# A graph-network pair on one core: x in a ring of four slots, loaded three groups ahead, the residual written over x, and the next group's statistics behind the second layer's

## The chip, the cores and the metric

One Trainium2 chip, one of its cores. The metric is the device time of one execution in microseconds (us); the kernel is timed in several runs, and one more execution is profiled. Engines: PE (TensorE, matmul and its weight loads PEld), DVE (VectorE), ACT (ScalarE), POOL (GpSimd) and SP (SyncE, which here only issues DMAs).

## The reference, cut to what matters

x is 128 graphs x 128 nodes x 512 features, float32; adj is one 128x128 0/1 matrix.

```
h   = relu(layernorm(x))
z_l, z_g = h @ W_lang.T, h @ W_grav.T
A_l = relu(cosine similarity of the rows of z_l) * not_eye
A_g = exp(-squared distance of the rows of z_g / (2 sigma^2)) * not_eye
K   = w * rows_to_sum_1(A_l * adj) + (1 - w) * rows_to_sum_1(A_g * adj)
x   = x + (K @ (h @ W_V.T)) @ W_O.T                    # first layer, with the residual
h   = relu(layernorm(x))
x   = x + adjacency-weighted sum of h over nodes + bias # second layer
```

## The kernel before, in words

Four graphs are a group (GB = 4), so there are 32 groups (NG). Every product is done in three passes on pairs of rounded parts (hi, lo), so each engine that empties a PSUM bank works in two steps: ACT copies the bank to the hi part, and DVE subtracts hi from the bank to make the lo part (`lo`, L553; the names y_lo, v_lo and hT_lo below are such subtractions). One iteration i of every engine's loop does, in PE's order:

1. **y**: eight products (60 matmuls of 512 columns) with h of group i against the Gram matrices of W_lang and W_grav, through a ring of four PSUM banks (`free` waits on `drained`, which DVE counts up); in front of the last, the transposes of K of group i-1.
2. **KV**: K times v of group i-1, 12 matmuls; DVE adds x to them (`residual`, L621, `add`, L629) and takes the layer norm's statistics (`stats`, L633).
3. **P**: 48 matmuls of 256 columns, similarities of group i, into p_ps; ACT copies it out in two halves (L434).
4. **v**: 48 matmuls, four banks; ACT copies (v_hi, L446), DVE makes v_lo. Between them ACT and DVE split h of the next group, which came back transposed (turned_hi, L401; turned_lo, L573: hT_lo). Behind b = 0 DVE sums the diagonal (sq, L723; sqc, L725), ACT shifts four tiles (L479), and behind b = 2 PE has transposed P and DVE adds it (L738).
5. **layer 1** (the second layer) of group i-1: four products of three matmuls; each waits for its h2_lo. DVE adds x_out to each bank (`output`, L675).

The order on each engine is written out by hand; there is no planner. Each engine waits on semaphores only, and runs its list in order. The b-th item of a name is written name(b) here.

POOL's list in an iteration: norm1 of group i+1 (ten small ops, L271 to L285), add_bias(0) and (1) of group i-1 (L295: x_out = x2 + bias, waits for the statistics bn2 of its b), norm2 of group i-1 (the same ten ops, waits for all four bn2), `diagonal` (L309: P_sb times a mask; waits for ACT's two copies of P), add_bias(2) and (3), row_norms (L315, L317), four h2_lo (L302: h2f minus h2_hi). ACT's h2_full (L467) makes h2f from x2 behind norm2's last op; h2_copy (L474) is h2_hi.

The statistics of x (`x_stats`, L558, bn_stats L565) are taken two groups ahead, by DVE in the v phase: for b 0 and 1 behind sqc, for b 2 and 3 behind hT_lo(1). The last two groups have none to take (`stats=False`, `after=False`).

x is loaded by SP into a ring of three slots, two groups ahead (`load_x(i + 2)`, one DMA of 1 MB). In an iteration SP issues: half of the 16 DMAs that move h's 32x32 blocks (`turn_h`; ACT issues the other half, L395), the load, the two DMAs that spread the norms, and four stores. h itself is transposed in blocks of 32 by DVE (L569); the DMAs then bring the blocks to h_turned, 32 partitions and 16 runs of 128 bytes each; there a partition's 16 runs lie behind each other, and the readers pick them with a strided pattern (`h_columns`).

Before the loop, the four weights are loaded into tiles that are free at that time: W_lang into x2, W_V into the ring's last slot.

## Time and profile before

| | us |
|---|---|
| three runs | 1314.11, 1312.95, 1311.78 (median 1312.95) |
| the profiled execution | 1311.88, of which the span of the profile 1310.1 |
| busy: PE, PEld | 1261.6, 1036.9 |
| busy: DVE, ACT, POOL | 1032.7, 704.4, 661.8 |
| granted clock of PE | 0.993 of full |
| moved by DMA | 112.55 MB, mean 86 GB/s |

A busy PE row counts matmuls that overlap in the pipeline. "Busy" is from the first part of the page; the chain of waits (fourth part, and a view of its own) goes from the last instruction back to what released it. In the views in order of time a line is: start in us from the span's start, duration in us, engine, line of the kernel, operation, output<-inputs, their shapes, how many instructions are merged in the line, and in brackets the idle time of the engine in front of it with what ended it. An engine's next instruction can be issued a little before the one in front has ended (bn_stats of 0.68 follow each other every 0.60), and one that is issued but can't start counts as running. "issue" is time in which nothing is waited for that the profile shows. An engine name with a q (SPq, ACTq) is its sequencer.

### The profile page before, as it was taken

Reading aid. Unit: us, or ns where it says so; the run is one execution under the profiler, and the core shown is the slowest. Engines: PE = TensorE matmul, PEld = TensorE weight load, DVE = VectorE, ACT = ScalarE, POOL = GpSimd, SP = SyncE. Lnnn points to the kernel's source line nnn. Section 1 sums busy time; section 2 is a strip of 40 time slices with the busy share of each in tenths; the row PEclk is TensorE's granted clock in tenths of the full one; section 3 lists DMA queues with packets and bytes.
Section 4 is the critical chain, followed back from the end, with each engine's and each line's share of the span. In section 5 each row is a group of like instructions: output and inputs, shape, how many; then the busy total and the mean of one; then the engine's idle time right before and its main releaser. Section 6 shows DMA issues by size and latency. Waiting matters only on the chain.

```text
span 1310.1 us, 22323 instructions
## 1 busy us (share of the span) xinstructions
PE 1261.6 (96%) x6324; PEld 1036.9 (79%) x6324; DVE 1032.7 (79%) x1733; ACT 704.4 (54%) x1324; POOL 661.8 (51%) x995
## 2 busy tenths in 40 slices
PE   7899999999999999999999999999999999999996
PEld 7777888777888777888887878887888877788874
DVE  5487777797777788777788777789777779777778
ACT  5346555456555456645456655555655545655533
POOL 1025654545664445664444665444565454566434
PEclk9999999999999999999999999999999999999997
DMA  5312433432333332343332243342243342233211
GB/s 203 65 36 78 105 72 96 104 72 75 101 88 87 98 82 70 96 104 73 96 98 63 87 104 72 96 104 65 79 104 72 96 104 70 76 102 81 59 38 64
DMA packets 308894, 112.55 MB, mean 86 GB/s; under 512 B 269840, under 2 KB 269968, under 8 KB 308880
## 3 DMA queue, kind: packets, MB, share of 16 engines
q1 hardware_dynamic: 177360, 95.78, 25.5%
q10 hardware_dynamic: 131520, 16.60, 7.7%
q8 instruction: 7, 0.11, 0.0%
q14 instruction: 7, 0.06, 0.0%
HBM read 46.20 MB, written 33.62 MB: 61 GB/s over the span
## 4 chain that ended last, share of the span: by engine, by line
PE 64%; DVE 17%; issue 11%; ACT 6%; DMA 1%; DVEq 0%; POOL 0%; ACTq 0%; SPq 0%
PE ring L856 49%; PE p_ps L856 14%; DVE hT_lo L573 5%; DVE sq L723 3%; ACT v_hi L446 3%; ACT chain L479 3%; DVE bn L565 2%; DVE x_out L675 2%; DVE v_lo L553 1%; DVE chain L738 1%; PE kt_ps L869 1%; DMA h2f<-in_L_gnn_W_grav 1%; ACT h L383 0%; DVE bn L633 0%; DVE y_lo L776 0%
## 5 line engine op out<-in xcount | busy, mean ns | idle before, releaser
L295 POOL TENSOR_TENSOR x_out<-x,bias_sb 128x512 f32<-128x512 f32 x128 | 176.5, 1400 | 468.2 <-DVE bn L633 468.2
L410 ACT ACTIVATE y_hi<-ring 128x512 fp32r<-128x512 f32 x256 | 148.4, 591 | 230.2 <-PE ring L856 227.4
L856 PE MATMUL ring<-hT_hi,Lw_hi 128*128 128x512 f32 x640 | 256.5, 401 | 6.6 <-DVE hT_lo L573 2.1
L856 PE MATMUL ring<-hT_hi,Lw_lo 128*128 128x512 f32 x640 | 250.4, 391 | 0.0
L856 PE MATMUL ring<-hT_lo,Lw_hi 128*128 128x512 f32 x640 | 249.8, 390 | 0.0
L553 DVE TENSOR_TENSOR v_lo<-ring,v_hi 128x512 fp32r<-128x512 f32 x128 | 87.4, 684 | 201.0 <-ACT v_hi L446 197.2
L856 PE MATMUL ring<-MT_hi,hT_hi 128*128 128x512 f32 x512 | 202.8, 396 | 0.0
L856 PE MATMUL ring<-MT_hi,hT_lo 128*128 128x512 f32 x512 | 199.8, 390 | 0.0
L856 PE MATMUL ring<-MT_lo,hT_hi 128*128 128x512 f32 x512 | 199.8, 390 | 0.0
L302 POOL TENSOR_TENSOR h_lo<-h2f,h_hi 128x512 fp32r<-128x512 f32 x124 | 172.7, 1422 | 45.4 <-ACT h_hi L474 45.4
L553 DVE TENSOR_TENSOR y_lo<-ring,y_hi 128x512 fp32r<-128x512 f32 x256 | 169.3, 681 | 29.6 <-ACT y_hi L410 29.5
L434 ACT ACTIVATE chain<-p_ps 128x512 f32<-128x512 f32 x64 | 38.2, 598 | 241.0 <-PE p_ps L856 241.0
L856 PEld LDWEIGHTS ring<-hT_hi,Lw_hi 128*128 128x128 f32 x640 | 120.2, 188 | 47.6 <-DVE x_out L675 16.1
L856 PE MATMUL p_ps<-y_hi,hT_lo 128*128 128x256 f32 x512 | 145.0, 283 | 0.0
L856 PE MATMUL p_ps<-y_lo,hT_hi 128*128 128x256 f32 x512 | 145.0, 283 | 0.0
L856 PE MATMUL p_ps<-y_hi,hT_hi 128*128 128x256 f32 x512 | 144.9, 283 | 0.0
L856 PEld LDWEIGHTS ring<-hT_hi,Lw_lo 128*128 128x128 f32 x640 | 120.2, 188 | 26.2
L856 PEld LDWEIGHTS ring<-hT_lo,Lw_hi 128*128 128x128 f32 x640 | 120.4, 188 | 21.7
L573 DVE TENSOR_TENSOR hT_lo<-h_turned,hT_hi 128x512 fp32r<-128x512 f32 x124 | 127.4, 1027 | 0.0
L856 PEld LDWEIGHTS ring<-MT_hi,hT_lo 128*128 128x128 f32 x512 | 96.2, 188 | 20.6
L856 PEld LDWEIGHTS ring<-MT_lo,hT_hi 128*128 128x128 f32 x512 | 96.5, 188 | 17.9
L856 PEld LDWEIGHTS ring<-MT_hi,hT_hi 128*128 128x128 f32 x512 | 96.4, 188 | 18.0
(163 smaller groups left out, 2555.8 us busy)
## 6 DMA issues: line engine op xcount, KB each, us to landing
x_ring<-in_x SPq DMA_DIRECT2D x32, 1024.0 KB, 5.7
out<-x_out SPq DMA_DIRECT2D x128, 256.0 KB, 2.2
h_turned<-h SPq DMA_DIRECT2D x248, 64.0 KB, 2.1
h_turned<-h ACTq DMA_DIRECT2D x248, 64.0 KB, 2.1
rn_cols<-rn_dram SPq DMA_DIRECT2D x31, 256.0 KB, 3.7
x<-in_L_gnn_W_lang SPq DMA_DIRECT2D x4, 256.0 KB, 5.3
h2f<-in_L_gnn_W_grav SPq DMA_DIRECT2D x1, 1024.0 KB, 8.9
chain<-in_L_gnn_W_O SPq DMA_DIRECT2D x1, 1024.0 KB, 12.6
```

The source lines that it names most:

```text
L295: pool.tensor_tensor(x_out[:, b], x2[:, b], bias_sb[:, :], ALU.add).then_inc(x2b_ready, 1)
L302: pool.tensor_tensor(h2[1][:, b], h2f[:, b], h2[0][:, b].bitcast(F32), ALU.subtract)\
L410: act.activation(y[0][:, a, :, l], bank(n).rearrange("p (b m) -> p b m", b=GB), ACT.Copy)\
L434: act.activation(P_sb[:, 2 * half:2 * half + 2], p_ps[:, 2 * half:2 * half + 2], ACT.Copy)\
L446: act.activation(v[0][:, b], bank(n), ACT.Copy).then_inc(hi_ready, 1)
L479: e = act.activation(P_sb[:, b, 1], P_sb[:, b, 1], ACT.Identity, bias=sq[:, b, 1:2])
L553: return dve.tensor_tensor(out, ps, part(hi), ALU.subtract)
L565: dve.bn_stats(bn1[:, b], xb).then_inc(bn1_done, 1)
L573: dve.tensor_tensor(hT_columns(1, b), h_columns(b), part(hT_columns(0, b)), ALU.subtract)\
L675: dve.tensor_tensor(x_out[:, b], bank(n), x_out[:, b], ALU.add).then_inc(drained, 1)
L723: dve.tensor_reduce(sq[:, :, :], diag, AX.X, ALU.add).then_inc(sq_ready, 1)
L856: mm = pe.matmul(out, lhsT, rhs, start=(k == 0), stop=(k == len(terms) - 1))
```

## The change

The ring of x gets a fourth slot, and group i+3 is loaded in iteration i, behind the stores. The residual is written over x in its slot; the tile x2 is gone, and add_bias, h2_full and the statistics read the slot (`x_rows`, whose address is computed from the group number in a register). On DVE the statistics of x move from the v phase into `residual`: one between stats(1) and stats(2), three behind stats(3); `added` is the wait for an add, now its own function, put two adds later. W_lang is loaded into the ring's slot 2. h_turned is laid out as [b, c, m] like a tile of h, so that the block DMAs write runs of 128 bytes 512 bytes apart, and both readers have a plain pattern. The prologue's loads of x are written out. The diff, where "..." marks what is left out:

```diff
@@ -12,7 +12,7 @@
 P = 128
 Q = 32
 GB = 4
-SLOTS = 3
+SLOTS = 4
 BANKS = 4
 EPS_LN = 1e-5
 EPS = 1e-8
@@ -70,7 +70,6 @@
         P_sb, diag, A = (chain[:, n] for n in range(3))
         K = sb("K", [P, GB, P])
         KT = [sb(f"KT_{s}", [P, GB, P], F32R) for s in ("hi", "lo")]
-        x2 = sb("x2", [P, GB, D])
         x_out = sb("x_out", [P, GB, D])
         h2f = sb("h2f", [P, GB, D])
         h2 = [sb(f"h2_{s}", [P, GB, D], F32R) for s in ("hi", "lo")]
@@ -101,10 +100,10 @@
         deg = sb("deg", [P, 4, GB, 2])
 
 
-        h_turned = sb("h_turned", [P, NQ, C * GB * Q])
+        h_turned = sb("h_turned", [P, GB, C, P])
         h_blocks = h[:, :, :].rearrange("p b (c j q) -> p j (b c) q", c=C, j=NQ)
 
-        raw_l = x2[:, :, :]
+        raw_l = x_ring[:, SLOTS - 2]
         raw_g = h2f[:, :, :]
         raw_v = x_ring[:, SLOTS - 1]
         raw_o = chain[:, 0:2].rearrange("p a b l m -> p (a b l m)").rearrange("p (c n) -> p c n", c=C)
@@ -182,13 +181,17 @@
                 eng.wait_ge(sem, count)
 
         def h_columns(b):
-            return h_turned[:, :, :].rearrange("p i (b c q) -> p b c i q", c=C, b=GB)[:, b]
+            return h_turned[:, b]
 
         def turned_to(i, j):
-            return h_turned[j * Q:(j + 1) * Q, i].rearrange("p (e q) -> p e q", q=Q)
+            return h_turned[j * Q:(j + 1) * Q, :, :, i * Q:(i + 1) * Q].rearrange("p b c q -> p (b c) q")
 
         def hT_columns(part, b):
-            return hT[part][:, :, b].rearrange("p c (i q) -> p c i q", q=Q)
+            return hT[part][:, :, b]
+
+        def x_rows(g, b):
+
+            return x_ring[:, bass.ds(g % SLOTS, 1), b].rearrange("p s d -> p (s d)")
 
         block = ctx.enter_context(nc.Block())
 
@@ -218,20 +221,15 @@
                     for j in range(NQ):
                         sp.dma_start(turned_to(i, j), h_blocks[i * Q:(i + 1) * Q, j]).then_inc(turned, 16)
 
-            def iteration(i, load=True, store=True, after=True):
+            def iteration(i, load=True, after=True):
                 if after:
                     turn_h(i + 1)
-                if load:
-                    sp.wait_ge(x_loaded, 16 * i + 32)
-                    if store:
-                        sp.wait_ge(drained, first_use(i) + G_USES + GB)
-                    else:
-                        sp.wait_ge(w_split, 3 * C)
-                    load_x(i + 2)
                 if after:
                     spread_norms(i)
-                if store:
-                    store_out(i - 1, first_use(i) + PER - GB)
+                store_out(i - 1, first_use(i) + PER - GB)
+                if load:
+                    sp.wait_ge(x_loaded, 16 * i + 48)
+                    load_x(i + 3)
 
             w_rows = w_lang.rearrange("(c p) n -> p c n", p=P)
             for c in range(C):
@@ -242,10 +240,18 @@
             sp.dma_start(raw_v, w_v.rearrange("(c p) n -> p c n", p=P)).then_inc(w_loaded["v"], 16)
             sp.wait_ge(x_loaded, 16)
             load_x(1)
-            iteration(0, store=False)
+            sp.wait_ge(w_split, C)
+            sp.wait_ge(x_loaded, 32)
+            load_x(2)
+            turn_h(1)
+            spread_norms(0)
+            sp.wait_ge(w_split, 3 * C)
+            sp.wait_ge(x_loaded, 48)
+            load_x(3)
             iteration(1)
-            with sp.Fori(2, NG - 2) as i:
+            with sp.Fori(2, NG - 3) as i:
                 iteration(i)
+            iteration(NG - 3, load=False)
             iteration(NG - 2, load=False)
             iteration(NG - 1, load=False, after=False)
             store_out(NG - 1, first_use(NG) + GB)
@@ -292,7 +298,7 @@
                 if b == 0:
                     wait_for(pool, out_stored, 16 * GB * g)
                 pool.wait_ge(bn2_done, GB * g + b + 1)
-                pool.tensor_tensor(x_out[:, b], x2[:, b], bias_sb[:, :], ALU.add).then_inc(x2b_ready, 1)
+                pool.tensor_tensor(x_out[:, b], x_rows(g, b), bias_sb[:, :], ALU.add).then_inc(x2b_ready, 1)
 
             def norm2(g):
                 std_factors(g, bn2, bn2_done, ln2, ln2_step)
@@ -379,8 +385,7 @@
                     elif not isinstance(g, int) or g > 1:
                         act.wait_ge(turned, TURN * (g - 1))
                 for b in range(b0, b0 + GB // 2):
-                    xb = x_ring[:, bass.ds(g % SLOTS, 1), b].rearrange("p s d -> p (s d)")
-                    act.activation(h[:, b], xb, ACT.Relu, bias=ln1[:, SHIFT, b:b + 1],
+                    act.activation(h[:, b], x_rows(g, b), ACT.Relu, bias=ln1[:, SHIFT, b:b + 1],
                                    scale=ln1[:, RSTD, b:b + 1]).then_inc(h_ready, 1)
 
             def t_hi(b, n):
@@ -464,7 +469,7 @@
                     act.wait_ge(ln2_step, LN_STEPS * (g + 1))
                 if b == 0:
                     wait_for(act, h2_split, GB * g)
-                act.activation(h2f[:, b], x2[:, b], ACT.Relu, bias=ln2[:, SHIFT, b:b + 1],
+                act.activation(h2f[:, b], x_rows(g, b), ACT.Relu, bias=ln2[:, SHIFT, b:b + 1],
                                scale=ln2[:, RSTD, b:b + 1]).then_inc(h2_done, 1)
 
             def h2_copy(g, b):
@@ -561,8 +566,7 @@
                     dve.wait_ge(x_loaded, 16 * g + 16)
                     wait_for(dve, ln1_step, LN_STEPS * g)
                 for b in range(b0, b1):
-                    xb = x_ring[:, bass.ds(g % SLOTS, 1), b].rearrange("p s d -> p (s d)")
-                    dve.bn_stats(bn1[:, b], xb).then_inc(bn1_done, 1)
+                    dve.bn_stats(bn1[:, b], x_rows(g, b)).then_inc(bn1_done, 1)
 
             def turn_blocks(g, b):
                 dve.wait_ge(h_ready, GB * g + b + 1)
@@ -618,32 +622,42 @@
                 dve.wait_ge(kt_hi, g + 1)
                 dve.tensor_tensor(KT[1][:, :, :], kt_ps[:, :, :], part(KT[0][:, :, :]), ALU.subtract).then_inc(kt_split, 1)
 
-            def residual(g, n, use, last=False):
+            def residual(g, n, use, x_next=None, last=False):
 
                 wait_for(dve, h2_done, GB * g)
                 wait_for(dve, x2b_ready, GB * g)
 
                 def add(b):
-                    xb = x_ring[:, bass.ds(g % SLOTS, 1), b].rearrange("p s d -> p (s d)")
                     dve.wait_ge(kv_done, GB * g + b + 1)
-                    dve.tensor_tensor(x2[:, b], bank(n + b), xb, ALU.add).then_inc(drained, 1)
+                    dve.tensor_tensor(x_rows(g, b), bank(n + b), x_rows(g, b), ALU.add).then_inc(drained, 1)
+
+                def added(b):
+                    dve.wait_ge(drained, use + b + 1)
 
                 def stats(b):
-                    dve.wait_ge(drained, use + b + 1)
-                    dve.bn_stats(bn2[:, b], x2[:, b]).then_inc(bn2_done, 1)
+                    dve.bn_stats(bn2[:, b], x_rows(g, b)).then_inc(bn2_done, 1)
 
                 if last:
                     for b in range(GB):
                         add(b)
+                        added(b)
                         stats(b)
                         if b % 2 == 1:
                             last_factors(b - 1, b + 1, b // 2 * LAST_STEPS)
                     return
                 add(0)
-                for b in range(1, GB):
+                add(1)
+                for b in range(2, GB):
+                    added(b - 2)
                     add(b)
-                    stats(b - 1)
-                stats(GB - 1)
+                    stats(b - 2)
+                added(GB - 1)
+                if x_next is not None:
+                    x_stats(x_next, 0, 1)
+                for b in range(GB - 2, GB):
+                    stats(b)
+                if x_next is not None:
+                    x_stats(x_next, 1, GB)
 
             def last_factors(b0, b1, before):
 
@@ -701,11 +715,12 @@
                         if before and n == G_USES - 1:
                             kt_lo(i - 1)
                 if before:
-                    residual(i - 1, n, first_use(i) + n)
+                    residual(i - 1, n, first_use(i) + n, i + 2 if stats and after else None)
                 else:
                     for c in range(C):
                         hi += 1
                         lo(MT[1][:, c], bank(n + c), MT[0][:, c], hi).then_inc(drained, 1)
+                    x_stats(i + 2, 0, GB)
                 n += GB
                 if not after:
                     last_chain(i, n, hi)
@@ -723,8 +738,6 @@
                         dve.tensor_reduce(sq[:, :, :], diag, AX.X, ALU.add).then_inc(sq_ready, 1)
                         dve.wait_ge(sq_ready, 2 * i + 1)
                         dve.tensor_scalar(sqc[:, :], sq[:, :, 0], EPS * EPS, None, ALU.max).then_inc(sq_ready, 1)
-                    if stats and b < 2:
-                        x_stats(i + 2, b * GB // 2, (b + 1) * GB // 2)
                     if b == 2:
                         sum_s(i)
                 if before:
```

## Rows read from the trace of the kernel before

**Rows 1.** The page's first part: busy time, share of the span, instructions.

```profile
PE 1261.6 (96%) x6324; PEld 1036.9 (79%) x6324; DVE 1032.7 (79%) x1733; ACT 704.4 (54%) x1324; POOL 661.8 (51%) x995
```

**Rows 2.** The chain of waits: start us, us, what (the KV matmuls of two groups).

```profile
600.35 3.01 PE ring L856 x12
...
639.35 3.01 PE ring L856 x12
```

**Rows 3.** PE in order of time, end of layer 1, start of y.

```profile
661.51 0.49 PE L856 MATMUL ring<-h_hi,A_hi 128*128 128x512 f32 x1 [0.22 <-POOL h_lo L302]
...
662.76 0.49 PE L856 MATMUL ring<-h_hi,A_hi 128*128 128x512 f32 x1 [0.29 <-POOL h_lo L302]
...
663.32 0.40 PE L856 MATMUL ring<-h_hi,A_lo 128*128 128x512 f32 x1
663.84 0.50 PE L856 MATMUL ring<-hT_hi,Lw_hi 128*128 128x512 f32 x1
```

**Rows 4.** POOL in order of time, the same group.

```profile
648.53 0.20 POOL L285 TENSOR_TENSOR ln<-ln 128x4 f32<-128x4 f32 x1
648.82 2.40 POOL L309 TENSOR_TENSOR chain<-chain,diag_of 128x1024 f32<-128x1024 f32 x1
651.17 1.29 POOL L295 TENSOR_TENSOR x_out<-x,bias_sb 128x512 f32<-128x512 f32 x1
...
657.06 5.57 POOL L302 TENSOR_TENSOR h_lo<-h2f,h_hi 128x512 fp32r<-128x512 f32 x4 [1.33 <-ACT h_hi L474]
```

**Rows 5.** DVE in order of time, the same group's v phase.

```profile
652.13 0.89 DVE L573 TENSOR_TENSOR hT_lo<-h_turned,hT_hi 128x512 fp32r<-128x512 f32 x1
...
656.58 0.68 DVE L573 TENSOR_TENSOR hT_lo<-h_turned,hT_hi 128x512 fp32r<-128x512 f32 x1
657.18 1.28 DVE L565 BATCH_NORM_STATS2 bn<-x_ring 128x6 f32 x2
...
658.97 1.26 DVE L573 TENSOR_TENSOR hT_lo<-h_turned,hT_hi 128x512 fp32r<-128x512 f32 x1
...
661.88 1.30 DVE L573 TENSOR_TENSOR hT_lo<-h_turned,hT_hi 128x512 fp32r<-128x512 f32 x1
663.10 1.28 DVE L675 TENSOR_TENSOR x_out<-ring,x_out 128x512 f32<-128x512 f32 x2
```

**Rows 6.** ACT in order of time, the same group.

```profile
650.89 0.60 ACT L446 ACTIVATE v_hi<-ring 128x512 fp32r<-128x512 f32 x1 [0.60 <-PE ring L856]
```

**Rows 7.** DVE and POOL in order of time, the same group's residual and norm2.

```profile
644.15 1.28 DVE L633 BATCH_NORM_STATS2 bn<-x 128x6 f32<-128x512 f32 x2
...
645.51 0.21 POOL L271 TENSOR_TENSOR ln<-bn 128x4 f32<-128x4 f32 x1 [0.41 <-DVE bn L633]
```

**Rows 8.** DVE and POOL in order of time, group 1.

```profile
98.13 1.28 DVE L633 BATCH_NORM_STATS2 bn<-x 128x6 f32<-128x512 f32 x2
...
102.65 2.39 POOL L309 TENSOR_TENSOR chain<-chain,diag_of 128x1024 f32<-128x1024 f32 x1
...
105.83 1.01 DVE L573 TENSOR_TENSOR hT_lo<-h_turned,hT_hi 128x512 fp32r<-128x512 f32 x1
```

**Rows 9.** DVE and PE in order of time, iteration 30 (`stats=False`).

```profile
1237.26 0.90 DVE L573 TENSOR_TENSOR hT_lo<-h_turned,hT_hi 128x512 fp32r<-128x512 f32 x1
...
1243.77 1.61 DVE L573 TENSOR_TENSOR hT_lo<-h_turned,hT_hi 128x512 fp32r<-128x512 f32 x1
...
1249.07 0.47 PE L856 MATMUL ring<-hT_hi,Lw_hi 128*128 128x512 f32 x1 [0.22 <-DVE x_out L675]
```

**Rows 10.** Who waited for whom: us in total, times, longest.

```profile
DVE bn L565 <- issue: 5.7, 28, 0.2
```

**Rows 11.** The page's sixth part: DMA issues, KB each, us to landing.

```profile
x_ring<-in_x SPq DMA_DIRECT2D x32, 1024.0 KB, 5.7
...
h_turned<-h ACTq DMA_DIRECT2D x248, 64.0 KB, 2.1
```

**Rows 12.** ACT in order of time, its block DMAs.

```profile
639.42 5.46 ACTq L395 DMA_DIRECT2D h_turned<-h  x8
```

## The prediction

> **What bounds the kernel now.** The page's first part comes first: TensorE (PE) is busy 1261.6 of 1310.1 us [rows 1], so a change pays only where PE stands still, and costs only where it makes PE wait. The chain of waits shows the period: the same 12 KV matmuls start at 600.35 and at 639.35 [rows 2], so one group takes 39.0 us. From here on the group that starts at 639.35 is read; the others look alike.
>
> PE's own timeline [rows 3] shows where it stands still. Its matmuls of 512 columns follow each other every 0.23 us. The products of the second layer (layer 1 in the code) for b = 2 and b = 3, at 661.51 and 662.76, have idle time in front of them that POOL's h2_lo ended; the last matmul of b = 3 starts at 663.32, yet the next group's first y matmul only at 663.84, 0.29 later than a pitch of 0.23 would have it: it waits for the bank that DVE's first x_out add empties. From 662.76 to 663.32 two matmuls take 0.56 instead of 0.46, so a restart costs 0.10 more.
>
> What sets these waits is a chain that runs backwards through three engines, and the reader should follow it in [rows 4 to 6]:
> - ACT's v_hi of b = 0 at 650.89, then two DVE splits, of which the second, hT_lo(0), is issued at 652.13 and takes 0.89;
> - DVE's sum of the diagonal (sq), ACT's four shifts, ACT's v_hi, hT_hi and h2_hi, and POOL's four h2_lo from 657.06, 5.57 long, to 662.63;
> - hT_lo(3), issued at 661.88, 1.30 long, and x_out(0), issued at 663.10, 0.74 in front of the y matmul, and 0.68 long.
>
> hT_lo is the interesting row. It is the same instruction four times a group, and takes 0.89, 0.68, 1.26, 1.30 [rows 5]. At 0.68 POOL is idle. In the other three POOL is in a large op: the x_out add of b = 2 runs 651.17 to 652.46 [rows 4], and hT_lo, issued at 652.13, ends 0.56 after that add, about the 0.60 pitch of an unhindered op. So hT_lo(0) starts when POOL's add is over, and **the end of hT_lo(0) is tied to POOL**: an add that starts later by t makes the chain later by t. Going one step back, that add follows the diagonal product (648.82, 2.40), which follows norm2 (its last op issued at 648.53) and ACT's second copy of P.
>
> The Trainium skill, "SBUF — State Buffer", section "SBUF: two separate sides", says that Vector and GpSimd share one pair of SBUF ports as an exclusive lock: a DVE op with two SBUF inputs and a GpSimd op that reads SBUF never run together, and the loser waits for the whole instruction. The trace agrees (0.68 alone, 1.30 behind a POOL op). If the ports were shared by bandwidth instead, a later POOL op would not push hT_lo(0)'s end one for one, and the sum below would be near nothing.
>
> **The change part by part.**
>
> *Statistics out of the v phase.* Four bn_stats, two pairs of 1.28, leave the stretch behind sq and the stretch in front of v_lo(2). The first pair stands beside ACT's shifts, and v_lo(1) waits for ACT: worth nothing. The second pair, 657.18 to 658.46 [rows 5], is on the printed chain. Does DVE get ahead without it? Iteration 30, the last but one, never had these statistics (there is no group 32), so the trace of before already shows it: hT_lo(2) is issued there at 1243.77 and takes 1.61, since POOL's second h2_lo is already running; from the end of hT_lo(0) to the y matmul it is 1238.16 to 1249.07, 10.91 us [rows 9], against 653.02 to 663.84, 10.82, with the statistics [rows 3, 5]. So removing them buys 0.0. The ends: at best the 0.29 by which y starts late behind layer 1's last matmul, plus the 0.10 of the restart, 0.39 a group; at worst 0.1 lost, as in that iteration. I take 0.
>
> *Statistics into the residual.* DVE now does add0, add1, add2, stats0, add3, stats1, the next group's x_stats(0), stats2, stats3, and then three more x_stats. Before, stats3 was the eighth op, now it is the ninth: one pitch of bn_stats later, 0.60 (two take 1.28, one 0.68) [rows 7]. The new waits `added(0)`, `added(1)`, `added(3)` ask for an op two or one places back, which is complete 0.68 after its start while the next slot comes 1.2 or 0.6 later; behind the last one four register ops follow. Before, the register work in front of x_stats left DVE idle 0.2 behind a short op [rows 10]; here it stands beside a 0.68 op, so 0, and 0.2 at most. Behind those waits are the later adds and statistics; who waits for them is POOL. The last three x_stats (1.8) lie in DVE's idle time during the P products, from 645.43 to the split behind v_hi(0) at about 651.5: 0.
>
> *What that does to POOL.* norm2 starts 0.08 after stats3's end (645.43 to 645.51) [rows 7], so it moves by 0.60, and so does its end. add_bias(0) and (1) also move, but end before stats3. The diagonal product has a little slack in front of it, as it also waits for ACT's copy of P, and group 1 is a natural trial of how much. There stats3 ends at 99.41 and hT_lo(0) is issued at 105.83, 6.42 apart, against 6.70 in the group read here: statistics 0.28 late. The diagonal product is 3.18 in front of hT_lo(0) instead of 3.31, so 0.13 late, and hT_lo(0) takes 1.01 instead of 0.89: 0.12 late [rows 8]. So 0.15 is absorbed and the rest arrives in hT_lo(0) whole. With 0.60: **0.45 us later per group.**
>
> *How far it travels.* hT_lo(0), sq, shifts, v_hi(1), h2_hi, the four h2_lo, layer 1 for b = 2 and 3, hT_lo(3), x_out, y: every link ends the wait of the next one, with PE idle at both ends, so 0.45 reaches the start of y. What has slack doesn't add: two h2_full of 0.8 behind norm2's end (648.73 + 0.60) are over at about 650.9, when v_hi(0) starts anyway; and should PE come to wait at the transposes of P for the later shifts, it would wait that much less at layer 1.
>
> *The residual over x, register addresses.* The same 128x512 operands in another tile; add_bias on POOL and h2_full on ACT get a register address. ACT's normalize and DVE's x_stats have one already, with no idle time but that 0.2 [rows 10]. 0; at most 0.1 a group on ACT behind ln2_step, which v_hi(0)'s slack holds.
>
> *x three groups ahead; SP's queue.* In the waits DVE's x_stats never wait for a load, only 0.2 each for issue [rows 10], so an earlier load frees nobody. On SP the load leaves its place between turn_h and spread_norms and goes behind the four stores, which follow the x_out adds (from 663.10, four of 0.6); with 5.7 to land [rows 11] it is there by about 672, while the next KV matmuls, near which the block DMAs run, start at 678.35, and x_stats ask for a load a whole group older. Its wait on x_loaded is long met, so turn_h behind it isn't held. Turn_h, spread_norms and the stores keep their instants. 0 (below: the last turn DMA lands a little sooner; above: nothing waits).
>
> *Layout of the moved blocks.* The same DMAs with the same 128-byte runs, landing in 2.1 [rows 11]; ACT's eight are out at 644.88 [rows 12], land by 647.0, and are read behind v_hi(0), after 650.9, so they could take 3.9 longer before anyone waits. hT_lo's strided read takes 0.68 when alone, the pitch of an op on 512 elements, so a plain read has nothing to save there. From below and above 0, and I take 0.
>
> *Prologue and end.* In group 0 x_stats(2) move in front of the P products, where DVE is idle; the v phase there waits for v_hi(3), PE's own. Two groups have no x_next, and their residual keeps its length. 0, within 1 us.
>
> **Sum.** x_next is there in groups 1 to 29: 29 x 0.45 = 13.1 us. The profiled execution took 1311.9 (span 1310.1), so 1325.0; it lies 1.1 below the median of the runs (1312.95), so I forecast 1326.0.
>
> **Rivals.**
> 1. *Faster: DVE was the bound.* If the order at the ports falls otherwise, so that hT_lo(2) and (3) don't stand behind h2_lo, y starts right behind layer 1: 29 x 0.39 = 11.3 us less, 1301.6. It decides only if POOL's delay stays under the 0.15 of slack. For it: the pair is on the printed chain. Against it: iteration 30 [rows 9]. Chance 0.1.
> 2. *No change: the delay is absorbed*, because hT_lo(0) gets the ports before POOL's add. hT_lo(0) is issued at 652.13, the add would be at 651.62, so the add's delay would have to be over 0.96 instead of 0.45, with v_hi(0) not held back (then hT_lo(0) takes 0.68). Near 1313. Chance 0.1.
> 3. *Much slower: the small POOL ops of norm2 now run beside x_stats*, and have to wait for them, by at most the 1.8 of three x_stats; half of it would be 0.9 more a group, 29 x 1.35 = 39, 1352. Against it: bn_stats has one SBUF input, and the pair at 657.18, issued while POOL's h2_lo runs, takes 1.28 as elsewhere [rows 4, 5, 7]. Or hT_lo(2) gets in front of h2_lo(1): of its 1.61 [rows 9] some 1.0 is waiting for an op of 1.3, so that op came only 0.3 earlier. h2_lo(3) would then be later by up to 0.6, of which the y start has 0.29 in hand: 0.3 a group more, 1335. Together 0.08.
> 4. *The change doesn't do what it says* (a load that still waits): there was no wait to remove; it is in the forecast.
>
> **Numbers.** Forecast 0.72, within it a delay between 0.2 (more slack than group 1 shows) and 0.8 (0.2 of bubble at the added wait, something on POOL): 29 x 0.2 = 6 to 29 x 0.8 = 23, that is 1319 to 1336. The range goes on to 1315 and 1338, towards rivals 2 and 3. A measurement of this kernel can tell about 0.2% (2.6 us) from no change. Faster by more 0.1, within 0.1, slower by more 0.8.
>
> **What would show it.** Right: period near 39.45; stats3 0.6 later against the KV matmuls; hT_lo(0) near 1.3; diagonal product issued 0.15 behind norm2's last op; layer 1's b = 2, 3 each still waiting for h2_lo, b = 2 by some 0.45 more; no gain from the v phase without bn_stats. Wrong: hT_lo(0) at 0.68 (rival 2), hT_lo(2), (3) at 0.68 and y right behind layer 1 (rival 1), norm2 longer than 3.2 (rival 3), or PE idle at a place where it isn't now.

## The result, and the profile after

The changed kernel takes 1328.07 us (median of four runs, 1327.02 to 1328.56) against 1313.46 for the kernel before: ratio 1.0112, 95% interval 1.0095 to 1.0130. It is 14.6 us slower. Forecast were 1326.0 and 1315 to 1338. The profiled execution took 1328.03, its span 1326.3. Two executions of the experiments further down, one of after_wait_hT (1367.76) and one of after_dve_h2lo_no_wait (2500.7), lay far above all the others of their kernels and are left out.

The page's first part of the changed kernel, busy time, answers [rows 1].

```profile
PE 1263.1 (95%) x6324; PEld 1033.6 (78%) x6324; DVE 1057.3 (80%) x1733; ACT 698.5 (53%) x1324; POOL 660.1 (50%) x995
```

PE does the same work in a span that is 16 us longer. DVE executes the same 1733 instructions and is busy 25 us longer; the costliest groups say with what (line engine op, out<-in, count, then busy us and mean ns of one):

```profile
L577 DVE TENSOR_TENSOR hT_lo<-h_turned,hT_hi 128x512 fp32r<-128x512 f32 x124 | 149.9, 1209 | 0.0
```

and of the kernel before

```profile
L573 DVE TENSOR_TENSOR hT_lo<-h_turned,hT_hi 128x512 fp32r<-128x512 f32 x124 | 127.4, 1027 | 0.0
```

124 times 182 ns is 22.5 of the 25 us. The waits (engine and line waited for, us in total, times, longest) show where PE lost its time; the changed kernel, then the kernel before:

```profile
PE ring L869 <- POOL h_lo L308: 30.2, 60, 0.7
```

```profile
PE ring L856 <- POOL h_lo L302: 16.1, 60, 0.3
```

The added 14.1 us lie where they were expected, in front of layer 1, and there in front of b = 2. In the chain, the KV matmuls of two groups answer [rows 2]:

```profile
647.54 3.02 PE ring L869 x12
...
687.05 3.02 PE ring L869 x12
```

The period is 39.51 instead of 39.00. From here on times inside a group are counted from its first KV matmul ("at 6.08"), so that kernels can be compared; group 15 is read throughout. First DVE, in order of time (start, us, instruction, count; residual and v phase, answering [rows 5, 7]):

```profile
648.74 1.97 DVE L632 TENSOR_TENSOR x_ring<-ring,x_ring 128x512 f32 x3
650.63 0.68 DVE L638 BATCH_NORM_STATS2 bn<-x_ring 128x6 f32 x1
651.23 0.67 DVE L632 TENSOR_TENSOR x_ring<-ring,x_ring 128x512 f32 x1
651.82 0.68 DVE L638 BATCH_NORM_STATS2 bn<-x_ring 128x6 f32 x1
652.42 0.68 DVE L569 BATCH_NORM_STATS2 bn<-x_ring 128x6 f32 x1
653.01 1.27 DVE L638 BATCH_NORM_STATS2 bn<-x_ring 128x6 f32 x2
654.20 1.86 DVE L569 BATCH_NORM_STATS2 bn<-x_ring 128x6 f32 x3
...
660.40 1.34 DVE L577 TENSOR_TENSOR hT_lo<-h_turned,hT_hi 128x512 fp32r<-128x512 f32 x1
...
665.31 0.68 DVE L577 TENSOR_TENSOR hT_lo<-h_turned,hT_hi 128x512 fp32r<-128x512 f32 x1
...
667.35 1.62 DVE L577 TENSOR_TENSOR hT_lo<-h_turned,hT_hi 128x512 fp32r<-128x512 f32 x1
...
670.62 1.28 DVE L577 TENSOR_TENSOR hT_lo<-h_turned,hT_hi 128x512 fp32r<-128x512 f32 x1
```

The pair stats2 and stats3 ends at 654.28, that is at 6.74; before at 6.08 (645.43 less 639.35). The one L569 in front of it is x_stats(0). Then POOL, answering [rows 4, 7]:

```profile
651.54 2.54 POOL L301 TENSOR_TENSOR x_out<-x_ring,bias_sb 128x512 f32<-128x512 f32 x2 [15.71 <-DVE bn L638]
654.36 0.20 POOL L277 TENSOR_TENSOR ln<-bn 128x4 f32<-128x4 f32 x1 [0.28 <-DVE bn L638]
...
657.38 0.20 POOL L291 TENSOR_TENSOR ln<-ln 128x4 f32<-128x4 f32 x1
657.54 2.40 POOL L315 TENSOR_TENSOR chain<-chain,diag_of 128x1024 f32<-128x1024 f32 x1
659.90 2.99 POOL L301 TENSOR_TENSOR x_out<-x_ring,bias_sb 128x512 f32<-128x512 f32 x2
...
665.78 5.57 POOL L308 TENSOR_TENSOR h_lo<-h2f,h_hi 128x512 fp32r<-128x512 f32 x4 [1.33 <-ACT h_hi L479]
```

The diagonal product is issued 0.16 behind the start of norm2's last op and stands at 10.00, before at 9.47; h2_lo(0) starts at 18.24, before at 17.71. Both are 0.53 late. ACT's timeline, answering [rows 6], has h2_full in front of v_hi(0) without idle time, so v_hi(0) starts at 11.64, 0.1 later than before, and waits no longer for PE but for its own engine:

```profile
657.76 1.52 ACT L472 ACTIVATE h2f<-x_ring,ln 128x512 f32 x2 [0.81 <-POOL ln L291]
659.18 0.58 ACT L451 ACTIVATE v_hi<-ring 128x512 fp32r<-128x512 f32 x1
```

PE's last waits answer [rows 3]:

```profile
670.24 0.49 PE L869 MATMUL ring<-h_hi,A_hi 128*128 128x512 f32 x1 [0.73 <-POOL h_lo L308]
...
671.49 0.50 PE L869 MATMUL ring<-h_hi,A_hi 128*128 128x512 f32 x1 [0.29 <-POOL h_lo L308]
...
672.56 0.50 PE L869 MATMUL ring<-hT_hi,Lw_hi 128*128 128x512 f32 x1
```

The wait for b = 2 grew from 0.22 to 0.73, that for b = 3 stayed at 0.29, and y starts at 25.02, before at 24.49.

Two distances tie these links together. In the eight kernels of this document in which hT_lo(0) stands behind the third bias add, it ends 0.55 behind the end of that add in every group from the second on but one, however long it had to wait. And in all twelve but one (before_dve_h2lo below) y starts 1.20 to 1.21 behind the end of POOL's last h2_lo: 24.49 less 23.28 before, 25.02 less 23.81 now.

**The sum.** First KV matmul at 94.23 instead of 93.12: 1.1. Then 29 groups at 0.51: 14.8. Behind them 0.3, of which 0.22 lie in iteration 30 (39.09 instead of 38.87), which takes no statistics of x but has the new order of adds. Together the 16.2 by which the spans differ. The 1.1 is not the change's: nearly all of it is TensorE's clock in the prologue. In both kernels PE stands still for 3.8 us before 46.5; the windows after that (stretch; us; PE PEld DVE ACT POOL busy; granted clock; DMA share; GB/s) are, of before,

```profile
46.50:49.90 3.40, 3.36 (x8) 2.74 (x9) 0.54 (x1) 0.00 (x0) 0.00 (x0) 0.52 1.16 187
49.90:52.30 2.40, 2.40 (x12) 1.93 (x12) 0.60 (x1) 0.60 (x1) 0.00 (x0) 1.00 0.92 192
```

and of the changed kernel

```profile
46.50:49.90 3.40, 3.20 (x8) 2.56 (x9) 0.69 (x2) 0.00 (x0) 0.00 (x0) 0.50 1.20 192
49.90:52.30 2.40, 2.40 (x8) 1.88 (x7) 0.00 (x0) 0.14 (x1) 0.00 (x0) 0.57 0.07 12
```

so the lower level of 1.2 GHz lasted longer: an estimate from the two clocks is 3.3 us before and 5.5 now, and 2.2 us at half the clock cost 1.1. It isn't tied to the kernel. In the five profiles with the prologue of before (before itself, one_more_stat, two_more_stats_b, before_lock_free, before_dve_h2lo) the first KV matmul starts at 93.12 to 94.70, in the seven with that of the changed kernel at 93.09 to 94.31.

### The profile page after: what moved, and what is told of

It is laid out like the page before. It is cut to its first block, busy times and chain, and to the rows that moved or that the text cites. A ratio compares the mean times of both kernels' runs of the same rounds, so it can differ in the third digit from the quotient of the medians.

```text
span 1326.3 us, 22484 instructions
## 1 busy us (share of the span) xinstructions
PE 1263.1 (95%) x6324; PEld 1033.6 (78%) x6324; DVE 1057.3 (80%) x1733; ACT 698.5 (53%) x1324; POOL 660.1 (50%) x995
## 4 chain that ended last, share of the span: by engine, by line
PE 44%; DVE 17%; issue 13%; POOL 11%; ACT 11%; POOLq 1%; DMA 1%; ACTq 1%; DVEq 0%; SPq 0%
PE ring L869 42%; DVE hT_lo L577 5%; POOL x_out L301 5%; ACT v_hi L451 3%; DVE sq L738 3%; ACT h_hi L479 3%; ACT chain L484 2%; POOL ln L289 2%; DVE v_lo L558 2%; DVE x_out L689 2%; DVE bn L638 2%; ACT h2f L472 2%; PE p_ps L869 1%; DVE chain L751 1%; PE kt_ps L882 1%
## 5 line engine op out<-in xcount | busy, mean ns | idle before, releaser
L301 POOL TENSOR_TENSOR x_out<-x_ring,bias_sb 128x512 f32<-128x512 f32 x128 | 176.0, 1396 | 496.2 <-DVE bn L638 496.2
L577 DVE TENSOR_TENSOR hT_lo<-h_turned,hT_hi 128x512 fp32r<-128x512 f32 x124 | 149.9, 1209 | 0.0
L472 ACT ACTIVATE h2f<-x_ring,ln 128x512 f32 (+1 forms) x128 | 97.2, 806 | 33.2 <-POOL ln L291 24.3
```

Source lines behind the costliest of these rows:

```text
L301: pool.tensor_tensor(x_out[:, b], x_rows(g, b), bias_sb[:, :], ALU.add).then_inc(x2b_ready, 1)
L472: act.activation(h2f[:, b], x_rows(g, b), ACT.Relu, bias=ln2[:, SHIFT, b:b + 1], scale=ln2[:, RSTD, b:b + 1]).then_inc(h2_done, 1)
L577: dve.tensor_tensor(hT_columns(1, b), h_columns(b), part(hT_columns(0, b)), ALU.subtract)\
```

## The experiments

All ratios are to the kernel before, measured on the same chip, with their 95% interval. The diffs show the edit that matters; "..." marks what is left out.

**one_more_stat: only the delay of stats3, on the kernel before.** One bn_stats that nobody reads, into a tile of its own, between stats1 and stats2 in groups 1 to 29; everything else is the kernel before.

```diff
                     add(b)
+                    if b == GB - 1 and g_has_more:
+                        dve.bn_stats(bn_spare[:, :], h2f[:, 0])
                     stats(b - 1)
```

> The kernel before with one thing added: in the residual of groups 1 to 29, between stats(1) and stats(2), one more bn_stats of 128x512 whose result nobody reads. Nothing else of the change is in it: three slots, x2, the statistics of x in the v phase, the old layout. Theory (stats3 one bn_stats later makes norm2, the diagonal product and POOL's third bias add later, and hT_lo(0) waits at the shared ports for that add): stats3 0.60 later, the diagonal product about 0.46 later, hT_lo(0) about 1.35 long instead of 0.89, period 39.0 + 0.46, 29 x 0.46 = 13.4 us more: about 1327. Rival (the loss comes from the statistics leaving the v phase, the layout, the ring or the order of loads): 1313 to 1315.

Measured 1325.46, ratio 1.0097 (1.0080 to 1.0114); period 39.45. Its POOL timeline (start, us, instruction, idle before and releaser) and its hT_lo(0) have the same picture as the change, with KV at 648.42 by the same count:

```profile
655.15 0.21 POOL L272 TENSOR_TENSOR ln<-bn 128x4 f32<-128x4 f32 x1 [1.02 <-DVE bn L634]
...
658.34 2.41 POOL L310 TENSOR_TENSOR chain<-chain,diag_of 128x1024 f32<-128x1024 f32 x1
```

```profile
661.20 1.35 DVE L574 TENSOR_TENSOR hT_lo<-h_turned,hT_hi 128x512 fp32r<-128x512 f32 x1
```

One op of 0.6 at this place, and nothing else, costs 0.44 a group (12.1 us in all): the size forecast for the whole change. (In the profile of this kernel one group, the second, is 1.2 longer still: there hT_hi(0) on ACT starts 1.3 late. The other groups and the other kernels don't show it at that size.)

**two_more_stats_b: does the delay go on one for one?** Two such ops, in the same place.

> As one_more_stat, with two bn_stats that nobody reads (each into a tile of its own) between stats(1) and stats(2) instead of one. The dose doubled, and a test of my second rival (beyond 0.96 of delay hT_lo(0) gets the ports before POOL's add). Theory: stats3 1.19 later, the diagonal product 1.05 later; h2_full, which stands in front of v_hi(0) on ACT, is 1.19 later too and pushes v_hi(0) and hT_lo(0) by about 0.5, so that the add still comes first; period 39.01 + 1.05 = 40.06, 1343 to 1344. Rival (hT_lo(0) slips in front of the add, 0.68 long): period about 39.5, 1328 or less.

Measured 1342.17, ratio 1.0222 (1.0205 to 1.0240), period 40.00: the second op costs 0.55 a group. The diagonal product stands at 10.50, the adds right behind it, and hT_lo(0) still waits:

```profile
667.70 3.01 POOL L297 TENSOR_TENSOR x_out<-x,bias_sb 128x512 f32<-128x512 f32 x2
```

```profile
668.07 1.48 DVE L575 TENSOR_TENSOR hT_lo<-h_turned,hT_hi 128x512 fp32r<-128x512 f32 x1
```

The add is issued before hT_lo(0) is and still goes first. The diagonal product is 1.03 late, more than the 0.96 from which rival 2 would decide, and the period still grows by 1.00: h2_full now holds v_hi(0) back, and hT_lo(0) with it (issued at 13.22, in one_more_stat at 12.79).

```profile
665.43 1.52 ACT L469 ACTIVATE h2f<-x,ln 128x512 f32<-128x512 f32 x2 [1.18 <-POOL ln L287]
666.85 0.58 ACT L448 ACTIVATE v_hi<-ring 128x512 fp32r<-128x512 f32 x1
```

**after_x_stats_last: only the place of x_stats(0), on the changed kernel.** All four x_stats stand behind stats3.

```diff
                 added(GB - 1)
-                if x_next is not None:
-                    x_stats(x_next, 0, 1)
                 for b in range(GB - 2, GB):
-                    stats(b)
+                    stats(b, SLOTS)
                 if x_next is not None:
-                    x_stats(x_next, 1, GB)
+                    x_stats(x_next, 0, GB)
```

(`stats(b, SLOTS)` names the same slot through g + 4.)

> The changed kernel, but all four statistics of the next x stand behind stats(3), so that stats(3) is the eighth op again. stats(0) still comes one add later than in the kernel before, so add_bias(0) and (1) on POOL are still about 0.8 late and end behind stats(3). Theory, as iteration 30 of the changed kernel shows it (diagonal product 0.25 late with stats(3) on time): norm2 starts behind add_bias(1), about 0.4 late, the diagonal product 0.25 to 0.3 late, period 39.3, about 1322. Rival A (only the ninth place of stats(3) matters, as my forecast had it): 1314 to 1316. Rival B (the place of the statistics is not it): 1328.

Measured 1317.89, ratio 1.0038 (1.0024 to 1.0052). Neither number was hit: 10.2 us come back, 4.4 stay. POOL's timeline shows why some stay:

```profile
647.22 2.55 POOL L301 TENSOR_TENSOR x_out<-x_ring,bias_sb 128x512 f32<-128x512 f32 x2 [15.72 <-DVE bn L638]
649.73 0.20 POOL L277 TENSOR_TENSOR ln<-bn 128x4 f32<-128x4 f32 x1
```

norm2 now has no idle time in front of it: stats3 is on time, but the second bias add is not over. The change had also put add2 in front of stats0, so that stats0 ends at 3.77 instead of 3.11 and the bias adds start 0.8 later (at 4.00 instead of 3.19). Before, they were

```profile
642.54 2.56 POOL L295 TENSOR_TENSOR x_out<-x,bias_sb 128x512 f32<-128x512 f32 x2 [14.90 <-DVE bn L633]
```

That is a second gate in front of norm2, hidden in the changed kernel behind the first, and worth 0.19 a group alone (period 39.20).

**after_stats_in_v: x_stats back in the v phase**, two and two as before; otherwise the kernel above (the diff is against it).

```diff
-                if x_next is not None:
-                    x_stats(x_next, 0, GB)
...
-                    x_stats(i + 2, 0, GB)
...
+                    if stats and b < 2:
+                        x_stats(i + 2, b * GB // 2, (b + 1) * GB // 2)
                     if b == 2:
```

> The changed kernel, but the statistics of x are back in the v phase, two pairs as in the kernel before. Four slots, the load, the residual over x, the layout and the order of adds stay. Theory (leaving the v phase buys nothing): the same time as the changed kernel with its statistics behind stats(3), about 1322, hT_lo(2) 1.26 instead of 1.6 long. Rival (emptying the v phase is worth up to 0.39 a group): about 11 us slower than that kernel, 1333.

Measured 1318.11, ratio 1.0045 (1.0028 to 1.0062), beside 1317.89 without them there. An empty v phase is worth nothing (period 39.20 in both), as [rows 9] had it.

**after_old_order: the old order of residual, everything else changed.** add0, add1, stats0, add2, stats1, add3, stats2, stats3, then four x_stats (the diff is against after_x_stats_last).

```diff
                 add(0)
-                add(1)
-                for b in range(2, GB):
-                    added(b - 2)
+                for b in range(1, GB):
                     add(b)
-                    stats(b - 2)
+                    added(b - 1)
+                    stats(b - 1, SLOTS)
                 added(GB - 1)
-                for b in range(GB - 2, GB):
-                    stats(b, SLOTS)
+                stats(GB - 1, SLOTS)
```

> The changed kernel with the residual's order as in the kernel before (add0, add1, stats0, add2, stats1, add3, stats2, stats3) and all four statistics of the next x behind it; each stats has its wait for its add. Everything else of the change stays: four slots, the load three groups ahead, the residual over x, the new layout, no statistics in the v phase. Theory: add_bias(0) starts as early as in the kernel before, but for about 0.1 of register work on POOL, stats(3) ends on time, norm2 and the diagonal product are on time, hT_lo(0) 0.9 long, period 39.02: 1313 to 1314.5, the same as before. Rival (some other part of the change costs too): 1318 or more, as in the two runs with the statistics out of the way.

Measured 1311.63, ratio 0.9992 (0.9983 to 1.0002), period 39.01. The diagonal product starts at 9.47, as before, and hT_lo(0) is that of before too:

```profile
653.20 0.90 DVE L577 TENSOR_TENSOR hT_lo<-h_turned,hT_hi 128x512 fp32r<-128x512 f32 x1
```

So the four slots, the earlier load, the residual over x, the register addresses, the new layout and the emptied v phase together cost nothing and bring nothing; **all of the 14.6 us are the order of DVE's adds and statistics in the residual**. It holds two causes that overlap, since norm2 waits for the later of the two: x_stats(0) in front of stats2 costs 0.44 a group alone (one_more_stat), add2 in front of stats0 0.19 alone (after_x_stats_last), both together 0.51.

**after_wait_hT: is it really the shared ports?** The changed kernel, with POOL's third bias add made to wait until hT_lo(0) is done. A wait more, and nothing less.

```diff
                 if before:
+                    if after:
+                        pool.wait_ge(ht_lo, GB * i + 1)
                     for b in range(GB // 2, GB):
                         add_bias(i - 1, b)
```

> The changed kernel with one wait more on POOL: the third bias add of a group is not issued before hT_lo(0) has ended. Nothing else moves; norm2 and the diagonal product are as late as in the changed kernel. Theory (the delay reaches PE only by way of the ports): hT_lo(0) 0.68 long, ending about 13.46 behind the KV matmuls instead of 14.20 (kernel before: 13.66), period about 38.8, 1313.5 + 1.1 - 29 x 0.2 = 1309, so 19 us faster than the changed kernel and a little faster than the kernel before. Rival (the delay travels by h2_full, the diagonal sum or the transposes of P instead): 1325 to 1328, with the wait at sq or v_hi(0) in place of hT_lo(0).

Measured 1312.05, ratio 0.9994 (0.9984 to 1.0004): a wait added to POOL makes the changed kernel some 16 us faster. Of its DVE and then its POOL:

```profile
652.33 0.68 DVE L579 TENSOR_TENSOR hT_lo<-h_turned,hT_hi 128x512 fp32r<-128x512 f32 x1
```

```profile
649.47 2.40 POOL L315 TENSOR_TENSOR chain<-chain,diag_of 128x1024 f32<-128x1024 f32 x1
653.28 2.55 POOL L301 TENSOR_TENSOR x_out<-x_ring,bias_sb 128x512 f32<-128x512 f32 x2 [1.41 <-DVE hT_lo L579]
...
657.30 5.49 POOL L308 TENSOR_TENSOR h_lo<-h2f,h_hi 128x512 fp32r<-128x512 f32 x4
```

The diagonal product is as late as in the changed kernel, hT_lo(0) takes the unhindered 0.68, and the delay is gone. It missed the 1309 expected because the pushed adds and the row norms now run without a gap into h2_lo(0), which starts at 17.82 although its h2_hi(0) on ACT ends at 17.51: POOL itself has become the limit.

**before_lock_free: the same relief for the kernel before.** The wait, and the fourth bias add behind the four h2_lo.

```diff
-                    for b in range(GB // 2, GB):
-                        add_bias(i - 1, b)
+                    if after:
+                        pool.wait_ge(ht_lo, GB * i + 1)
+                    add_bias(i - 1, 2)
...
                         h2_lo(i - 1, b)
+                    add_bias(i - 1, 3)
```

> The kernel before with two edits on POOL: the third bias add waits for the end of hT_lo(0), and the fourth comes behind the four h2_lo, so that row_norms and h2_lo aren't late for it. Theory (the end of hT_lo(0) is tied to POOL through the ports, and PE's waits at layer 1 and y hang on it): hT_lo(0) 0.68, ending about 0.2 earlier, h2_lo(0) and y 0.2 to 0.3 earlier, period 38.75, about 1305.5. Rival (in the kernel before the ports don't set the end, something else with the same time does): 1313.

Measured 1310.09, ratio 0.9979 (0.9969 to 0.9988). hT_lo(0) takes 0.68 and y starts 0.18 earlier, but of that only 0.08 of the period is left (38.93). The waits show where the rest goes:

```profile
PE ring L858 <- DVE KT_lo L621: 6.2, 29, 0.2
```

In the kernel before PE has no such wait. The timelines of this kernel lead back from it: the fourth bias add now stands in front of norm1 of the next group, whose last op ends at 29.22 instead of 27.29; behind it ACT's h and its four K are late (34.06 instead of 33.14), and DVE's sum for K, which waits for all four, starts at 34.10, only 0.09 earlier than before. This is read from the traces; no run tests it.

**after_dve_h2lo: is there a use for the emptied v phase?** after_old_order, the wait for hT_lo(0) and, of POOL's four h2_lo, the first one on DVE behind hT_lo(1), with a semaphore of its own.

```diff
+                    if after:
+                        pool.wait_ge(ht_lo, GB * i + 1)
...
-                    for b in range(GB):
+                    for b in range(1, GB):
                         h2_lo(i - 1, b)
...
                     turned_lo(i + 1, b)
+                    if before and b == 1:
+                        h2_lo_0(i - 1)
```

> Built on after_old_order and the wait for hT_lo(0) on POOL: the first of the four h2_lo of a group goes from POOL to DVE, into the place that the statistics left, behind hT_lo(1). Theory (the end of the group is set by POOL's four h2_lo and the ports, not by DVE's amount of work): POOL does three, h2_lo(3) ends near 22.6 behind the KV matmuls instead of 23.3, y starts near 23.85 instead of 24.49, period about 38.4, 1295. Rival (DVE's own list sets the start of y): no gain, 1311 to 1314.

Measured **1287.85**, ratio 0.9816 (0.9799 to 0.9832), better than expected; period 38.16. Its DVE, its POOL and its PE at the end of layer 1:

```profile
644.61 0.68 DVE L580 TENSOR_TENSOR hT_lo<-h_turned,hT_hi 128x512 fp32r<-128x512 f32 x1
645.21 0.69 DVE L687 TENSOR_TENSOR h_lo<-h2f,h_hi 128x512 fp32r<-128x512 f32 x1
...
646.65 0.96 DVE L580 TENSOR_TENSOR hT_lo<-h_turned,hT_hi 128x512 fp32r<-128x512 f32 x1
```

```profile
645.61 4.42 POOL L308 TENSOR_TENSOR h_lo<-h2f,h_hi 128x512 fp32r<-128x512 f32 x3 [0.26 <-ACT h_hi L482]
```

```profile
650.16 0.49 PE L876 MATMUL ring<-h_hi,A_hi 128*128 128x512 f32 x1
...
651.24 0.50 PE L876 MATMUL ring<-hT_hi,Lw_hi 128*128 128x512 f32 x1
```

DVE's op takes 0.69 where POOL's takes 1.4, and the last h2_lo ends at 22.47, 0.8 earlier than the 23.28 before; b = 1 and 2 gain as much. PE no longer waits in front of b = 2 and starts b = 3 0.13 behind that end, and y starts at 23.68, 1.21 behind it as ever: POOL still sets it.

**before_dve_h2lo: the same two edits in the kernel before**, whose v phase still holds the four x_stats.

> The kernel before with the same two edits (wait for hT_lo(0) on POOL, first h2_lo on DVE), the statistics of x still in the v phase. Theory (leaving the v phase is worth nothing alone, but worth something once DVE has a piece of POOL's work there): DVE now reaches hT_lo(2) about 1 later, sum and v_lo(3) behind it, y near 24.4, 1311, so about 16 us slower than after_dve_h2lo. Rival (the statistics in the v phase cost nothing there either): as after_dve_h2lo, 1295.

Measured 1309.78, ratio 0.9974 (0.9964 to 0.9984). In its DVE and PE timelines the second pair of statistics stands behind the moved op, the last split of v comes later, and PE waits for that one instead:

```profile
657.67 0.69 DVE L677 TENSOR_TENSOR h_lo<-h2f,h_hi 128x512 fp32r<-128x512 f32 x1
658.28 1.27 DVE L568 BATCH_NORM_STATS2 bn<-x_ring 128x6 f32 x2
```

```profile
663.22 0.50 PE L867 MATMUL ring<-h_hi,A_hi 128*128 128x512 f32 x1 [0.58 <-DVE v_lo L556]
```

So the moved statistics, worth nothing while POOL sets the end of layer 1, are worth 22 us once DVE does. (The two kernels also differ in the slots, the load, the layout and the addresses, which after_old_order shows to be worth nothing in the old schedule; in this one they were not tried apart.)

**after_dve_h2lo_no_wait: that kernel without the wait for hT_lo(0).**

> As after_dve_h2lo, but without the wait that holds POOL's third bias add behind hT_lo(0): what is that wait's share of the 25 us? Theory (hT_lo(0) ends 0.2 later behind POOL's add, and the chain from it to y is still what sets the period): hT_lo(0) 0.9 long, y 0.2 later than in after_dve_h2lo, period 38.16 + 0.2 x (0.1 to 0.2 of it kept), 1291 to 1294. Rival (POOL's three h2_lo now start behind ACT's h2_hi whatever hT_lo(0) does): 1288.

Measured 1294.58, ratio 0.9854 (0.9832 to 0.9876), just above the range expected: hT_lo(0) is back at 0.89, and 0.2 a group (period 38.37) makes most of the 6.7 us between the two.

## Why the prediction was right

- **The mechanism held.** stats3 late, norm2 late, diagonal product late, the add in front of hT_lo(0) late, and through it all of the second half of the group. one_more_stat has only that and costs 0.44; after_wait_hT has all of it but the order at the ports and costs nothing. hT_lo(0) was forecast near 1.3 and took 1.34; "diagonal product issued 0.15 behind norm2's last op": 0.16; the wait of b = 2 "by some 0.45 more": 0.51.
- **0.45 a group was 0.51.** Delay and slack were each slightly off. stats3 is 0.66 late, not 0.60: add2 waits at `added(0)` and starts 0.08 late, a wait that I had costed at 0 with 0.2 as its upper end. norm2 follows it by the same 0.08. Of the 0.66, 0.13 are absorbed, not 0.15. 29 times 0.06 is 1.7 of the 2.1 us by which the forecast is short. The forecast also put the last two groups at nothing; iteration 30 costs 0.22 for the order of its adds.
- **"add_bias(0) and (1) also move, but end before stats3"** was true by 0.2 and hid something: with stats3 on time they are the gate, at 0.19 a group. It changes nothing in the forecast, but I would have been wrong about any smaller version of this change, as my 1322 for after_x_stats_last was, in size.
- **Statistics out of the v phase buy 0.0**: shown, by after_stats_in_v beside after_x_stats_last, and as read from the iteration that never had them. The reason given (POOL ends last there) is shown by before_dve_h2lo.
- **Slots, load, SP's queue, in-place residual, register addresses, layout: 0**: shown together, by after_old_order at 0.9992. One by one they weren't tried. One bound in it was wrong: ACT was to lose at most 0.1 behind ln2_step. From the end of norm2 to the start of h2_full it is 0.18 in the changed kernel and 0.04 before, so 0.14.
- **Prologue "within 1 us"**: it was 1.1 in the profiled executions, nearly all of it the clock.
- **Rival 1** (faster) needed hT_lo(2) and (3) free of h2_lo; they take 1.62 and 1.28. **Rival 2** (absorbed) needed hT_lo(0) at the ports first; it is not even at twice the delay, since its condition ("v_hi(0) not held back") fails first. That is also where I was too sure: h2_full is not "over when v_hi(0) starts anyway" but, with the 0.14 of the register address on top of the delay, holds it by 0.1 already in the changed kernel, unseen because hT_lo(0) waits for the ports in any case. **Rival 3** (norm2 beside x_stats): norm2 takes 3.02 from first to last issue in both kernels, with three x_stats beside it now.
- The median lies 2 us over the forecast and inside the range. That it is so near is not luck in the mechanism, which the runs bear out link by link, but the 0.45 rests on the slack read from one group, and with a smaller first delay the second gate, which the forecast did not have, would have made it wrong.

## What to carry to other kernels

Before an instruction is put "into a free place" of an engine's order, look which instructions behind it feed another engine, and move it behind the last of them: here one 0.6 us statistic in front of the two that POOL waited for cost 10 to 12 us of 1313, and the same statistic one pair later nothing. If two engines share ports, the order in which they come matters more than the length of either op, and a wait that makes the uncritical one come second can pay: 16 us in the changed kernel, 6.7 in after_dve_h2lo, but 3 in the kernel before, with its fourth add moved as well. Work taken off an engine that isn't the bound brings nothing by itself; fill the room with a piece of the bounding engine's work in the same change, which here, with the old order and the wait, turned +14.6 us into some -25.

## What the runs showed that was not expected

- A semaphore wait for an op that started 1.3 us earlier, together with register work, is not free on DVE: add2 starts 0.68 behind add1 instead of 0.60. No run separates the two. On POOL and ACT an address from a register behind a wait costs 0.14 to 0.15: from stats0's end to the bias add 0.23 in the changed kernel and 0.08 before, from norm2's end to h2_full 0.18 and 0.04. It is the same in after_old_order, 0.23 and 0.18.
- A bn_stats is not hindered by POOL's large ops and doesn't hinder them: the pair takes 1.28 beside h2_lo [rows 5], three take 1.86 beside norm2's small ones. A DVE op with two inputs in SBUF is: hT_lo takes 0.68 alone, up to 1.77 behind h2_lo (after_wait_hT). v_lo, which reads one of its two inputs from a PSUM bank, takes 0.67 to 0.69 beside h2_lo too. The Trainium skill, "SBUF — State Buffer", section "SBUF: two separate sides", says that DVE's own pair of ports never waits for anyone, and that whichever op starts first on the shared pair has it for the whole instruction. The traces agree on both: 1.28 beside h2_lo for the statistics, 1.77 for the split.
- Small POOL ops pay for it too: L277 on 128x4 takes 0.66 in after_wait_hT beside hT_lo(3), and 0.20 behind stats3, where DVE has only statistics. And one input doesn't keep every DVE op out of it: sqc, a TENSOR_SCALAR on 128x4, takes 0.17 in the kernel before and 0.43 in after_wait_hT, where it ends 0.02 behind POOL's bias add.
